# First loads and the slots of all operations rearranged, and the low halves of the FFN's relu outputs moved from VectorE to POOL, in a two-layer cross-attention kernel

## Chip, cores and metric

The kernel runs on one core of a Trainium2 chip. The metric is the device time of one execution in microseconds; the time of the kernel before is the median of 3 runs.

## What is computed

`x` (64 x 128 x 256, f32) goes through two layers, each a cross-attention and a feed-forward part, each on the layer-normed `x` and added to it:

```python
x = x + L0_xattn(_layernorm(x), ctx, ctx, mask, ...)
x = x + L0_ffn(_layernorm(x), W1, b1, W2, b2)
x = x + L1_xattn(_layernorm(x), ctx, ctx, _lenS2, ...)
x = x + L1_ffn(_layernorm(x), W_base, ..., Wa_up, ba_up)

def _quantize(W):                      # in L0_ffn, EPS = 1e-5
    gamma = jnp.mean(jnp.abs(W))
    return jnp.clip(jnp.round(W / (gamma + EPS)), -1.0, 1.0)
h = jax.nn.relu(jnp.einsum('bsd,fd->bsf', x, Wq1) + b1)
out = jnp.einsum('bsf,df->bsd', h, Wq2) + b2
```

Attention has 16 heads of 16 over 128 keys; layer 0 masks scores by an integer mask, layer 1 by a length for each sequence. The second feed-forward part has 8 experts: for each it reconstructs the input, takes the expert of the smallest loss for each sequence, and adds that expert's adapter to a dense base.

## The kernel before

The 64 sequences are worked in 32 pairs (256 rows of `x` each), and everything of a pair has one place in a fixed timetable. Each engine runs the same loop `for t in range(FIRST, END)`, with FIRST = -14 and END = 16 * 31 + 79, and in it lines `for p in at(t, o)`: operation `o` of pair `p` is issued in slot t = 16 p + o. So 16 slots are one pair's period, and up to six pairs are in work at once. Slots are an order and no clock: each engine runs its list in order, waits by semaphores (`Signal.done`), and a late operation holds all that stand behind it. The timetable is written out by hand for TensorE (PE), VectorE (DVE), ScalarE (ACT), GpSimd (POOL) and SyncE (SP, which issues all DMAs).

The stages of pair p and their slots on TensorE: keys and `count` -11, `turn(0)` (transpose of the normed x) -7, `queries(0)` -6, then by DMA through a scratch in DRAM (`spill`, `stack`) into `qs` and `ks`; `scores(0, j)` 0 to 7, `scores_t(0, j)` 6 to 13, `mix(0, u)` 9 to 15, `output(0)` 17, `turn(1)` 20, `ffn_up` 22 to 24, `ffn_down` 28 and 29, then the same attention for layer 1 from 33 to 58, experts from 61 on, `up` 75.

- Scores are made twice. `scores` goes to VectorE for the row maxima (`maximum`, L818; in layer 0 four custom instructions with the mask's bias, L831, in layer 1 one reduction, L823). `split_max` (L836) writes them as f16 pairs, `maxima` (L354) on SyncE puts these as two more rows into `qs` by four small DMAs, and `scores_t` (L1147), with the maxima in the product, goes to ACT for the exponential (`exps`, L593). In layer 0 POOL multiplies the result by the mask (`apply_mask`, L502) before `mix` (L1159).
- The first FFN wants its f32 activations as two f16 parts. `relus` (L616) on ACT writes `work` (two buffers), `h_highs` (L630) the f16 value, and `h_lows` (L882) on VectorE the rest, `work - high`. The relu of the third and fourth piece waits until both have read the buffer. Keys and queries are split in the same way (`high` on ACT, `low` on VectorE, L794).
- POOL also makes rstd and the normalised x of four stages (`rstd_of` L462, `normalise` L484), the mask's parts and bias, and adds the biases of two projections (`add_bias`).
- PSUM has one bank for scores, one for transposed scores, one for `mix`, and five for all else (`BANKS`, L54): each name there, as T0 (`turn(0)`), F1_0 to F1_3 (`ffn_up`), O0 (`output(0)`), lives in one bank, and TensorE may start a name only when the reader of the bank's last name is done.

Head: SyncE loads pair 0 and the EARLY weights, the lengths, the two FFN weights (1 MB each) and the fifteen LATE weights, then constant rows of `qs` and `ks` (nine DMAs from a DRAM row, L392 and L395), and only then enters the loop. VectorE sums |W| of the FFN weights at t = 0 (L1062), POOL reduces the sums over partitions (L556), and VectorE quantises in ten steps at t = 2 to 11 (`quantise`, L744).

Of the kernel before, what the change touches and what calls it, by code (L numbers as in the profile page):

```python
# [86 lines left out]
def build(nc, x, lens, mask, mask_t, wq0, bq0, wk0, bk0, wv0, bv0, wo0, bo0, w1t, b1, w2t, b2,  # L87
          wq1, wk1, wv1, wo1, w_base, wd1, bd1, wd2, bd2, adapters, ctx_in, out):
    with ExitStack() as ctx:
# [109 lines left out]
        const_dram = dram("const_dram", [3, T], F16)  # L199
# [79 lines left out]
        rows_loaded = sem("rows_loaded")  # L279
# [30 lines left out]
        def _(sp):  # L310
            def load(p, ahead=False):
                if p == 0 and not ahead:
                    return
# [19 lines left out]
            def stack(l, j, p):  # L333
# [7 lines left out]
                sp.wait_ge(scr_written[l][j], 16 * (p + 1))  # L341
                for n in range(4):
# [1100 lines left out]
```

## Time and profile before

| | us |
|---|---|
| median of 3 runs | 1799.05 |
| lowest, highest | 1795.69, 1802.66 |
| profiled execution | 1797.68 |
| its span | 1795.7 |
| TensorE busy | 1595.8 |
| VectorE busy | 1491.1 |
| ACT busy | 903.7 |
| POOL busy | 977.2 |

The profile is one execution. The span runs from its first to its last instruction, and the execution's own time is 2.0 us longer. Busy times are of instructions in work; an engine's sequencer and issued DMAs do not count. A view of waits says before which instruction an engine stood idle and what released it; where several semaphores are waited for, it names the one that came last by the profile, which can be the wrong one. `L` numbers are lines of the kernel before.

### The profile page before, as it was taken

The numbers are of one execution on the slowest core, as the hardware profiler recorded it, in microseconds if no ns is written. First come the engines' busy times: TensorE is split into PE (matmuls) and PEld (weight loads), VectorE is DVE, ScalarE is ACT, GpSimd is POOL, SyncE is SP. The second block draws the span as 40 slices with busy tenths as digits, with TensorE's granted clock in tenths as the row PEclk, the third lists the DMA queues.
The fourth block names the chain that finished last, engine by engine and source line by source line (L and its number), as shares of the span: only waits on it lengthen the run. The fifth ranks groups of instructions, "written<-read, shape, count | busy, mean of one in ns | idle before, by whom it ended". The sixth has DMA issues, their size and how long they took to land.

```text
span 1795.7 us, 44012 instructions
## 1 busy us (share of the span) xinstructions
PE 1595.8 (89%) x15136; PEld 1290.6 (72%) x15136; DVE 1491.1 (83%) x5215; ACT 903.7 (50%) x2465; POOL 977.2 (54%) x1069
## 2 busy tenths in 40 slices
PE   2467999999999999999999999999999999999875
PEld 1355777787777777877777778777777787777654
DVE  2667798988889998888899998888899989888652
ACT  0123455555555555555555655555556555555542
POOL 2456655655565656555666565556665655564200
PEclk9879999999999999999999999999999999999987
DMA  6345456554554564555545655555546555542311
GB/s 172 57 65 91 87 85 105 93 90 93 96 84 85 92 105 93 90 93 95 88 79 94 105 98 85 93 99 90 77 89 105 97 90 89 99 83 50 57 35 30
DMA packets 286501, 157.32 MB, mean 88 GB/s; under 512 B 38964, under 2 KB 281928, under 8 KB 286280
## 3 DMA queue, kind: packets, MB, share of 16 engines
q1 hardware_dynamic: 286280, 154.51, 49.1%
q8 instruction: 121, 1.98, 0.6%
q14 instruction: 100, 0.82, 0.2%
HBM read 111.44 MB, written 41.96 MB: 85 GB/s over the span
## 4 chain that ended last, share of the span: by engine, by line
PE 52%; DVE 26%; issue 10%; DMA 5%; SPq 4%; POOL 2%; ACT 2%; POOLq 0%; DVEq 0%; ACTq 0%
PE psD L1182 7%; DVE dump L831 6%; PE psD L1214 5%; PE psD L1203 5%; PE psV L1170 4%; PE psD L1224 4%; PE psD L1118 4%; PE psD L1129 4%; PE psS L1143 4%; PE psX L1155 4%; DVE dif L902 3%; PE psD L1248 3%; DMA qs<-scr 2%; PE psD L1089 2%; DVE hhl L884 2%
## 5 line engine op out<-in xcount | busy, mean ns | idle before, releaser
L603 ACT ACTIVATE pT<-psX 128x512 f32<-128x512 f32 x512 | 305.4, 596 | 406.1 <-PE psX L1155 404.6
L506 POOL TENSOR_TENSOR pT<-pT,keep 128x512 f32<-128x512 f32 x256 | 334.5, 1312 | 94.3 <-ACT pT L603 86.9
L465 POOL TENSOR_SCALAR veps<-mv 128x2 f32<-128x2 f32 x128 | 28.9, 226 | 589.7 <-DVE mv L776 589.7
L491 POOL TENSOR_SCALAR xn<-xr,mv,rstd 128x256 f32<-128x256 f32 x256 | 312.1, 1226 | 7.3 <-POOL rstd L475 0.2
L831 DVE CUSTOM_DVE_ANT_0 dump<-psS,bias 128x128 bf16<-128x128 f32 x1024 | 234.3, 284 | 40.3 <-PE psS L1143 39.1
L823 DVE TENSOR_REDUCE mx<-psS 128x4 f32<-128x512 f32 x256 | 173.2, 677 | 102.5 <-PE psS L1143 100.7
L1143 PE MATMUL psS<-ks,qs 65*128 65x128 f16 x2048 | 204.4, 223 | 56.5 <-DMA qs<-scr 38.0
L647 ACT ACTIVATE dif<-dif 128x256 f32<-128x256 f32 x512 | 206.5, 408 | 75.6 <-DVE dif L902 75.4
L902 DVE SCALAR_TENSOR_TENSOR dif<-psD,bd2s,xT 128x256 f32<-128x256 f32 x512 | 213.1, 470 | 14.3 <-PE psD L1224 13.6
L1155 PE MATMUL psX<-qs,ks 67*128 67x128 f16 x2048 | 201.9, 221 | 20.0 <-ACT pT L603 15.5
L1143 PEld LDWEIGHTS psS<-ks,qs 65*128 65x128 f16 x2048 | 146.1, 99 | 99.1 <-issue 29.4
L1155 PEld LDWEIGHTS psX<-qs,ks 67*128 67x128 f16 x2048 | 142.3, 98 | 70.8 <-ACT pT L603 27.8
L1170 PE MATMUL psV<-pT,v 128*32 128x128 f32 x4096 | 171.7, 287 | 14.0 <-POOL pT L506 10.7
L1224 PE MATMUL psD<-hd,wd2s 64*128 64x256 f32 x1024 | 144.9, 401 | 13.9 <-DVE xr L875 12.4
L1182 PE MATMUL psD<-wo,attT 128*128 128x256 f32 x512 | 138.5, 418 | 13.1 <-DVE attT L866 13.0
L1170 PEld LDWEIGHTS psV<-pT,v 128*32 128x32 f32 x4096 | 99.6, 112 | 60.8 <-issue 36.5
L627 ACT ACTIVATE work<-psD,b1s 128x256 f32<-128x256 f32 x256 | 104.4, 488 | 72.4 <-PE psD L1195 57.2
L1106 PE MATMUL psD<-ctxT,wk 128*128 128x256 f32 x512 | 125.1, 388 | 12.2 <-DVE bqr L938 12.2
L1195 PE MATMUL psD<-xs,w1q 128*128 128x256 f16 x1024 | 133.8, 274 | 0.1
L1118 PE MATMUL psD<-xT,wq 128*128 128x256 f32 x512 | 132.1, 395 | 0.7 <-ACT xT L576 0.7
L1129 PE MATMUL psD<-wv,ctxT 128*128 128x256 f32 x512 | 131.5, 401 | 0.0
L1089 PE MATMUL psD<-ident,xn 128*128 128x128 f32 x512 | 83.2, 286 | 54.0 <-ACT work L627 46.6
(101 smaller groups left out, 3177.1 us busy)
## 6 DMA issues: line engine op xcount, KB each, us to landing
scr<-packed SPq DMA_DIRECT2D x128, 256.0 KB, 2.8
ks<-scr SPq DMA_DIRECT2D x256, 128.0 KB, 4.5
qs<-scr SPq DMA_DIRECT2D x256, 128.0 KB, 4.6
adapter<-in_adapters SPq DMA_DIRECT2D x64, 192.5 KB, 2.7
xr<-in_x SPq DMA_DIRECT2D x32, 256.0 KB, 2.8
ctxT<-in_ctx SPq DMA_DIRECT2D x32, 256.0 KB, 3.1
qs<-mrows SPq DMA_DIRECT2D x512, 2.0 KB
out_y<-xr SPq DMA_DIRECT2D x32, 256.0 KB, 5.0
```

The lines of the kernel that those rows point to most:

```text
L491: nc.gpsimd.tensor_scalar(xn[:, XN[s], b], xr[:, p % NX, b], mv[:, s, b, 0:1], rstd[:, s, b:b + 1], ALU.subtract, ALU.mult).then_inc(norme ...
L506: nc.gpsimd.tensor_tensor(blk, blk, keep[:, p % 2, j // 4].unsqueeze(1).to_broadcast([P, 4, P]), ALU.mult).then_inc(masked.sem, 1)
L603: nc.scalar.activation(pT[:, j % 4], X[:], ACT.Exp, scale=SCALE).then_inc(exp_done[l].sem, 1)
L647: nc.scalar.activation(blk, blk, ACT.Square, accum_out=acc[:, e, b:b + 1]).then_inc(squared.sem, 1)
L831: ins = nc.vector.tensor_tensor_reduce(out=dump[:, a], in0=S[:, a * P:a * P + P], in1=bias0[:, p % 2, b], scale=1.0, scalar=-3e38, op0=ALU ...
L902: nc.vector.scalar_tensor_tensor(out=dif[:, e % 4, k], in0=bank[f"rec{e}"][:, k * T:k * T + T], scalar=bd2s[:, e, k:k + 1], in1=xT3[:, p % ...
L1118: ins = nc.tensor.matmul(dst[:, m * T:m * T + T], wq[l][:, k, m * P:m * P + P], src[:, k], start=(k == 0), stop=(l == 1 and k == KD - 1))
L1143: ins = nc.tensor.matmul(S[:, a * P:a * P + P], qs[0:MASK_ROW + 1, r, h, t0:t0 + P], ks[0:MASK_ROW + 1, r, h, t0:t0 + P], start=True, stop ...
L1155: ins = nc.tensor.matmul(X[:, a * P:a * P + P], ks[0:ROWS, r, h, t0:t0 + P], qs[0:ROWS, r, h, t0:t0 + P], start=True, stop=True)
L1170: ins = nc.tensor.matmul(V[32 * a:32 * a + 32, (2 * half + s) * P:(2 * half + s) * P + P], v2[l][:, b, half * UH + 2 * a + s], pT[:, (2 * ...
L1182: ins = nc.tensor.matmul(dst[:, b * D:b * D + D], attT[:, l, b, k], wo[l][:, k], start=(k == 0), stop=(k == KD - 1))
L1224: ins = nc.tensor.matmul(dst[s][:, k * T:k * T + T], wd2s[half, m, k * P:k * P + P], hd[half, m], start=True, stop=True)
```

## The change

Four things change at once.

1. *Head.* Pair 1 is loaded ahead (`load(1, True)`); the rows of constants in `qs` and `ks` are written by one memset on POOL and one on VectorE, each 3 partitions x 6144 words, in place of the nine DMAs; the LATE loads are issued inside the loop, one a slot from t = -4 on; the |W| sums, the length steps and the POOL reduction move from t = 0 to t = -6, the ten quantising steps from t = 2 to 11 together to t = -2.
2. *Slots.* Nearly every operation on all five engines has another slot or another place within it; END is 16 * 31 + 77.
3. *Banks.* The five shared PSUM banks hold other groups of names.
4. *Low halves.* `h_lows` is an instruction of POOL.

```diff
-END = BODY * (NP - 1) + 79
+END = BODY * (NP - 1) + 77
 BANKS = (
-    ("rec2", "cnt", "rec0", "rec7", "down", "up"),
-    ("rec4", "v0", "F1_1", "T2", "O1"),
-    ("O0", "k1", "T1", "rec5", "F2", "rec1", "loss"),
-    ("F1_3", "hd1", "rec3", "k0", "q1", "T3"),
-    ("q0", "v1", "T0", "rec6", "F1_0", "F1_2", "hd0"),
+    ("cnt", "rec5", "v1", "hd0", "q0"),
+    ("v0", "q1", "T2", "F1_1", "T0", "hd1", "T3"),
+    ("O0", "F1_2", "rec1", "loss", "rec7", "up"),
+    ("O1", "k0", "rec6", "rec3", "F2", "down", "rec0"),
+    ("rec2", "F1_0", "T1", "k1", "F1_3", "rec4"),
 )
...
-                for dst, src in LATE:
-                    sp.dma_start(dst, src).then_inc(w_late, 16)
-                sp.wait_ge(len_steps, 4)
-                sp.dma_start(len_dram, len_rows[:]).then_inc(len_stored, 16)
-                sp.wait_ge(len_stored, 32)
-                for n in range(NR):
-                    sp.dma_start(qs[MASK_ROW:MASK_ROW + 1, n], const_dram[1:2].unsqueeze(1).to_broadcast([1, H, T]))\
-                        .then_inc(rows_loaded, 16)
-                    for k in range(2):
-                        sp.dma_start(ks[MASK_ROW + 1 + k:MASK_ROW + 2 + k, n],
-                                     const_dram[2:3].unsqueeze(1).to_broadcast([1, H, T])).then_inc(rows_loaded, 16)
+            load(1, True)
...
+                if LATE_SLOT <= t < LATE_SLOT + len(LATE):
+                    dst, src = LATE[t - LATE_SLOT]
...
+                        sp.dma_start(dst, src).then_inc(w_late, 16)
...
+            nc.gpsimd.memset(qs[MASK_ROW:MASK_ROW + 3].rearrange("p r h t -> p (r h t)").bitcast(F32), pair16(BIG16))\
+                .then_inc(q_rows_set, 1)
...
+            def h_lows(p, j):
+                h_high.done(pool, p, j)
+                nc.gpsimd.tensor_tensor(hhl[:, 1, 2 * j:2 * j + 2], work[:, j % 2], hhl[:, 0, 2 * j:2 * j + 2],
+                                        ALU.subtract).then_inc(h_low.sem, 1)
...
-            def h_lows(p, j):
-                h_high.done(dve, p, j)
-                nc.vector.tensor_tensor(hhl[:, 1, 2 * j:2 * j + 2], work[:, j % 2], hhl[:, 0, 2 * j:2 * j + 2],
-                                        ALU.subtract).then_inc(h_low.sem, 1)
...
+            nc.vector.memset(ks[MASK_ROW:MASK_ROW + 3].rearrange("p r h t -> p (r h t)").bitcast(F32), pair16(M_UP))\
+                .then_inc(rows_set, 1)
...
-                for p in at(t, 23):
-                    h_lows(p, 0)
```

In the rows below every line is one instruction, or several alike, in the order in which the engine issues them, with the semaphores it waits for in brackets.

TensorE, from the last pieces of `ffn_up` (L1195) to `turn(0)` (L1089) and `mix` (L1170), before:

```order
L1195 MATMUL psD<-xs,w1q 128x256 [waits h_relu]
L1195 MATMUL psD<-xs,w1q 128x256 x7
L1143 MATMUL psS<-ks,qs 128x128 [waits stacked10,max_done0]
L1143 MATMUL psS<-ks,qs 128x128 x3
L1195 MATMUL psD<-xs,w1q 128x256 [waits k_low0]
L1195 MATMUL psD<-xs,w1q 128x256 x7
L1089 MATMUL psD<-ident,xn 128x128 [waits normed0,h_relu]
L1089 MATMUL psD<-ident,xn 128x128 x3
L1170 MATMUL psV<-pT,v_0 32x128 [waits masked,turned1]
L1170 MATMUL psV<-pT,v_0 32x128 x7
```

and now (L1130 keys, L1180 `scores_t`, L1168 `scores`, L1220 `ffn_up`, L1195 `mix`, L1113 `turn(0)`):

```order
L1130 MATMUL psD<-ctxT,wk 128x256 [waits ctx_loaded1,h_relu]
L1130 MATMUL psD<-ctxT,wk 128x256 x3
L1180 MATMUL psX<-qs,ks 128x128 [waits exp_done0]
L1180 MATMUL psX<-qs,ks 128x128 x3
L1168 MATMUL psS<-ks,qs 128x128 [waits stacked10,max_done0]
L1168 MATMUL psS<-ks,qs 128x128 x3
L1220 MATMUL psD<-xs,w1q 128x256 [waits loss_out]
L1220 MATMUL psD<-xs,w1q 128x256 x7
L1195 MATMUL psV<-pT,v_0 32x128 [waits masked,turned1]
L1195 MATMUL psV<-pT,v_0 32x128 x7
L1113 MATMUL psD<-ident,xn 128x128 [waits normed0,h_relu]
L1113 MATMUL psD<-ident,xn 128x128 x3
```

`mix` now stands ahead of `turn(0)`, and the fourth piece of `ffn_up` has moved behind it. The `h_relu` for which `turn(0)` waits was that of F1_2, the third piece; now it is that of F1_1.

POOL, from the first mask of layer 0 (L506, `apply_mask`) to the fourth or fifth, before:

```order
L506 TENSOR_TENSOR pT<-pT,keep 128x512 [waits exp_done0]
L459 TENSOR_SCALAR bias<-mqf,allc 128x128 [waits max_done0,mask_q]
L459 TENSOR_SCALAR bias<-mqf,allc 128x128
L506 TENSOR_TENSOR pT<-pT,keep 128x512 [waits exp_done0] x2
L498 TENSOR_TENSOR xr<-xr,bob 128x512 [waits normed0]
L498 TENSOR_TENSOR xr<-xr,b2b 128x512 [waits normed1]
L506 TENSOR_TENSOR pT<-pT,keep 128x512 [waits exp_done0]
```

and now (L523 `apply_mask`, L528 `h_lows`, L476 bias, L515 `add_bias`):

```order
L523 TENSOR_TENSOR pT<-pT,keep 128x512 [waits exp_done0] x2
L528 TENSOR_TENSOR hhl<-work,hhl 128x512 [waits h_high]
L476 TENSOR_SCALAR bias<-mqf,allc 128x128 [waits max_done0,mask_q]
L476 TENSOR_SCALAR bias<-mqf,allc 128x128
L523 TENSOR_TENSOR pT<-pT,keep 128x512 [waits exp_done0]
L528 TENSOR_TENSOR hhl<-work,hhl 128x512 [waits h_high]
L523 TENSOR_TENSOR pT<-pT,keep 128x512 [waits exp_done0]
L515 TENSOR_TENSOR xr<-xr,b2b 128x512 [waits normed1]
L515 TENSOR_TENSOR xr<-xr,bob 128x512 [waits normed0]
L528 TENSOR_TENSOR hhl<-work,hhl 128x512 [waits h_high] x2
L523 TENSOR_TENSOR pT<-pT,keep 128x512 [waits exp_done0]
```

Four low halves of the pair before stand between the first mask and the fifth, two of them back to back.

SyncE in the head, from the last row copies (L392, L395) to the first pair's stacks (L344), before:

```order
L392 DMA qs<-const_dram 1x16x256
L395 DMA ks<-const_dram 1x16x256 x2
L330 DMA scr<-packed 128x4x256 [waits k_low0,k_high0]
L344 DMA ks<-scr 16x16x256 [waits scr_written01]
L344 DMA ks<-scr 16x16x256 x3
L351 DMA ks<-const_dram 1x16x256
L330 DMA scr<-packed 128x4x256 [waits q_low0,q_high0]
L344 DMA qs<-scr 16x16x256 [waits scr_written00]
```

and now, from the early load of pair 1 (L327 to L334) on (L341 `spill`, L361 and L368 `stack`):

```order
L327 DMA xr<-in_x 128x2x256
L330 DMA ctxT<-in_ctx 128x512
L333 DMA mq_ld<-in_mask 128x2x128 [waits mask_k,mask_q]
L334 DMA mt_ld<-in_mask_t 128x2x128
L341 DMA scr<-packed 128x4x256 [waits k_low0,k_high0]
L361 DMA ks<-scr 16x16x256 [waits rows_set,len_stored,scr_written01]
L361 DMA ks<-scr 16x16x256 x3
L368 DMA ks<-const_dram 1x16x256
L341 DMA scr<-packed 128x4x256 [waits q_low0,q_high0]
L361 DMA qs<-scr 16x16x256 [waits scr_written00]
L361 DMA qs<-scr 16x16x256 x3
```

The spills of pair 0 now follow the loads of pair 1 directly; the LATE loads and the lengths' row come behind the second stack.

In the steady loop SyncE still issues `spill(0, 1, p + 1)` ahead of `maxima(0, p, 1)` (slots 9 and 10, before both 8), while on VectorE `low(0, 1, p + 1)` moves from before the eighth maximum, `maximum(0, p, 7)`, to behind the `split_max(0, p, 1)` that follows it.

## Rows read from the trace of the kernel before

**Rows 1.** The page, part 1: busy us (share) xinstructions
```profile
PE 1595.8 (89%) x15136; PEld 1290.6 (72%) x15136; DVE 1491.1 (83%) x5215; ACT 903.7 (50%) x2465; POOL 977.2 (54%) x1069
```

**Rows 2.** Windows: busy us of each engine, PEclk, DMA share, GB/s
```profile
913.27:937.15 23.88, 21.75 (x218) 18.11 (x216) 22.45 (x59) 12.56 (x28) 16.78 (x15) 1.00 0.47 67
800.00:1000.00 200.00, 189.65 (x1858) 154.86 (x1856) 179.69 (x625) 110.79 (x302) 121.26 (x132) 0.99 0.54 91
```

**Rows 3.** Timeline of TensorE: `count` of pairs 7 and 32
```profile
297.03 0.27 PE L1096 MATMUL psD<-mtb,onesb 128*128 128x256 bf16 x1
...
1577.86 0.27 PE L1096 MATMUL psD<-mtb,onesb 128*128 128x256 bf16 x1
```

**Rows 4.** The view of the waits from 500 to 1500 us: total, times, longest
```profile
POOL veps L465 <- DVE mv L776: 310.4, 58, 10.1
...
PE psD L1089 <- ACT work L627: 33.6, 20, 1.8
...
PE psD L1224 <- DVE xr L875: 7.9, 19, 0.4
```

**Rows 5.** Timelines of TensorE, ACT and VectorE, one steady pair
```profile
918.68 0.38 PE L1143 MATMUL psS<-ks,qs 65*128 65x128 f16 x4
...
921.56 0.65 PE L1089 MATMUL psD<-ident,xn 128*128 128x128 f32 x4 [1.62 <-ACT work L627]
...
925.58 0.39 PE L1155 MATMUL psX<-qs,ks 67*128 67x128 f16 x4
...
920.67 0.84 ACT L627 ACTIVATE work<-psD,b1s 128x256 f32<-128x256 f32 x2 [1.98 <-PE psD L1195]
...
915.96 0.82 DVE L800 SCALAR_TENSOR_TENSOR packed<-psD,bks,packed 128x256 f16<-128x256 f32 x2
...
917.66 0.98 DVE L838 TENSOR_SCALAR m<-mx 128x16 f16<-128x16 f32 x1
...
919.02 1.57 DVE L884 TENSOR_TENSOR hhl<-work,hhl 128x512 f16<-128x512 f32 x1
```

**Rows 6.** Timelines of SyncE's queue and of VectorE, head: first pair's spills
```profile
37.01 0.51 SPq L330 DMA_DIRECT2D scr<-packed  x1
...
41.90 0.53 SPq L330 DMA_DIRECT2D scr<-packed  x1
...
26.87 0.69 DVE L805 TENSOR_TENSOR packed<-psD,packed 128x512 f16<-128x512 f32 x1 [7.10 <-ACT packed L590]
```

**Rows 7.** Timelines of TensorE, VectorE and POOL, head: around the first scores
```profile
52.93 0.61 PE L1143 MATMUL psS<-ks,qs 65*128 65x128 f16 x4 [26.73 <-DMA qs<-scr]
...
54.43 2.28 DVE L1062 TENSOR_REDUCE gam<-dif 128x1 f32<-128x2048 f32 x1
56.62 2.28 DVE L1062 TENSOR_REDUCE gam<-hhl 128x1 f32<-128x2048 f32 x1
...
63.59 0.30 DVE L776 BATCH_NORM_AGGREGATE mv<-stats 128x2 f32<-128x6 f32 x2
...
66.38 0.89 POOL L449 TENSOR_SCALAR mqf<-mq_ld 128x256 f32<-128x256 int32 x1 [6.99 <-issue]
```

**Rows 8.** Timeline of VectorE, head: a memset
```profile
1.83 0.91 DVE L931 MEMSET v<- 128x1024 f32 x1 [0.16 <-issue]
```

**Rows 9.** Lines with shapes apart, 400 to 1600 us: busy, mean ns
```profile
L506 POOL TENSOR_TENSOR pT<-pT,keep 128x512 f32<-128x512 f32 x190 | 244.9, 1294 | 69.3 <-ACT pT L603 63.7
...
L884 DVE TENSOR_TENSOR hhl<-work,hhl 128x512 f16<-128x512 f32 x96 | 84.0, 896 | 0.0
...
L498 POOL TENSOR_TENSOR xr<-xr,bob 128x512 f32<-128x512 f32 x24 | 41.0, 1710 | 0.0
```

**Rows 10.** SyncE queue in a steady pair; chain of waits at 152 us
```profile
917.88 0.39 SPq L330 DMA_DIRECT2D scr<-packed  x1
919.12 2.69 SPq L358 DMA_DIRECT2D qs<-mrows  x4
...
152.50 1.70 DMA qs<-mrows
```

More of the change, by code:

```diff
@@ L311, in load @@
             def load(p, ahead=False):
-                if p == 0 and not ahead:
+                if p < 2 and not ahead:
                     return
@@ L693, in _ @@
                     exps(0, p, 0)
-                for p in at(t, -10):
+                for p in at(t, 22):
+                    relus(p, 0)
+                for p in at(t, -9):
                     high(0, 1, p)
@@ L1006, in _ @@
                     turn_out(1, p, 1)
-                for p in at(t, -9):
-                    low(0, 1, p)
                 for p in at(t, 7):
@@ L1039, in _ @@
                     split_max(1, p, 0)
+                for p in at(t, -4):
+                    low(0, 0, p)
+                for p in at(t, 12):
+                    turn_out(0, p, 0)
                 for p in at(t, 44):
@@ L1267, in _ @@
                     mix(1, p, 0)
-                for p in at(t, 33):
-                    turn(2, p)
+                for p in at(t, 49):
+                    scores_t(1, p, 3)
                 for p in at(t, 1):
@@ L1273, in _ @@
                     output(0, p)
-                for p in at(t, 49):
-                    scores_t(1, p, 3)
+                for p in at(t, 33):
+                    turn(2, p)
                 for p in at(t, 2):
                     scores(0, p, 2)
-                for p in at(t, 66):
-                    reconstruct(p, 2)
                 for p in at(t, 50):
@@ L1282, in _ @@
                     mix(1, p, 1)
+                for p in at(t, 66):
+                    reconstruct(p, 2)
                 for p in at(t, 3):
@@ L1288, in _ @@
                     queries(1, p)
+                for p in at(t, 68):
+                    reconstruct(p, 3)
+                for p in at(t, 52):
+                    mix(1, p, 2)
                 for p in at(t, 4):
                     scores(0, p, 4)
+                for p in at(t, 20):
+                    turn(1, p)
                 for p in at(t, 52):
                     scores_t(1, p, 6)
-                    mix(1, p, 2)
-                for p in at(t, 68):
-                    reconstruct(p, 3)
-                for p in at(t, 4):
+                for p in at(t, 5):
                     values(0, p)
-                for p in at(t, 20):
-                    turn(1, p)
+                for p in at(t, 53):
+                    scores_t(1, p, 7)
+                for p in at(t, -11):
+                    count(p)
                 for p in at(t, 5):
@@ L1303, in _ @@
                     keys(0, p)
-                for p in at(t, 53):
-                    scores_t(1, p, 7)
-                for p in at(t, -11):
-                    count(p)
-                for p in at(t, 6):
-                    scores(0, p, 6)
                 for p in at(t, 22):
@@ L1374, in _ @@
                     scores(1, p, 6)
-                    scores_t(1, p, 0)
                 for p in at(t, 62):
                     hidden(p, 0)
+                for p in at(t, 46):
+                    scores_t(1, p, 0)
+                for p in at(t, 47):
+                    scores(1, p, 7)
                 for p in at(t, 63):
```

267 lines of the change are left out of this document (143 added, 124 removed).

## The prediction

> **What bounds the kernel now.** I read the page first: TensorE is busy 89% of the span, VectorE 83% [rows 1]. Shares of a span hide its stages, so the windows come next. In the middle TensorE works 189.65 of 200 us at a granted clock of 0.99, its level of 2.4 GHz, while POOL works 121 [rows 2]. The `count` matmul is issued once a pair and gives the period: from the seventh pair's to the last one's are 25 periods in 1280.8 us, **51.23 us a pair** [rows 3]. At 189.65/200 TensorE's own work is 48.6 us of it, so at most 2.65 us a pair can be won in the steady part. Then the waits, over 1000 us or 19.5 pairs: TensorE stands 33.6 us for ACT's relu (1.72 us a pair) and 7.9 us for VectorE (0.4); POOL stands 310 us, 15.9 a pair, for moments [rows 4]. Last the timelines. The longest TensorE wait is that of the `turn(0)` transpose, 1.62 us [rows 5]. Its bank holds the relu's input, and the relu starts at 920.67, right behind the end of VectorE's low half (919.02 + 1.57). The view of the waits names TensorE as what released the relu, but the time fits the low half, which frees `work`. So a full VectorE queue, through ACT, stops TensorE once a pair.
>
> The head has its own limit. SyncE issues all fifteen LATE loads and the row copies ahead of the first spill, which goes only at 37.01, the second at 41.90, though VectorE had finished the second's data at 27.56 (26.87 + 0.69) [rows 6]. The first scores start at 52.93 after 26.73 us of idle. Then VectorE does two reductions (2.28 us each) between the maxima, and POOL, behind its all-reduce, stands 6.99 us for nothing that the profile shows before it prepares the second pair at 66.38; the second pair's moments had been ready at 63.9 [rows 7].
>
> **The change part by part.** The sum is made against the profiled execution, 1797.68 us (span 1795.7 and 2.0 around it); the median of the runs is 1.4 higher.
>
> *First scores.* LATE loads and row copies leave the way of the spills; rows of constants are set by memsets. The second spill can go at about 27.6 instead of 41.90, that is 14.3 us. VectorE's memset of 6144 words would take 6 x 0.91 = 5.5 us [rows 8], in a gap where it waits for the bias of the queries anyway. POOL's memset of the same size at the same price ends near 8 us, before the moments; at twice the price it would push the chain by 1 to 2 us, inside the lower end. The statistics no longer stand behind the length steps, which starts the query chain some 3 us earlier, but `any_of` and the gamma reductions (4.6 us) now stand before the low half of the queries on VectorE and hold most of that back. I take 1.2 us more: **15.5 us**. From spill to first scores stay 11.0 us (41.90 to 52.93). Ends: 9.3 us if the second MB-sized weight load and the early second pair slow the spills by 5 us; 17.3 if all 3 us come through. Quantising moves ahead of the first maxima, into that 11 us of DMA: its ten steps are cheap beside this, and its cover is just long enough.
>
> *Second pair.* The reductions (4.56 us) leave the maxima, and the 6.99 us stand falls into the time before the first scores. POOL will then start the second pair's rstd when its moments are ready rather than 4.3 us later (66.38 and two mask instructions, 1.8, against 63.9, [rows 7]). 4.56 + 4.3 = **8.9 us**; ends 4.6 and 11.5 (both stalls whole). LATE loads now come between later slots; their first user is the output projection of slot 17, so I cost them at nothing, covered by some 50 us. If that cover failed, the first FFN would wait.
>
> *Low halves to POOL.* VectorE loses 4 instructions of 0.896 us a pair, POOL gains 4. A POOL instruction with two SBUF inputs of this size takes 1.294 us [rows 9]: +5.2 us a pair on an engine with 15.9 idle. No trace row has it with an f16 input; ends 0.9 (VectorE's own time) and 2.6 us (twice the row), taken 1.3 since shape and form are the row's. The relus of slot 9 now wait for POOL's `h_lows`, which follows the mask of slot 7 directly, and the transpose's bank is held by F1_1, whose relu has no such wait; before the transpose TensorE has keys, scores, a further `ffn_up` and `mix`, over 3 us. So the 1.72 us wait goes: **-1.7 us a pair**. VectorE's 3.6 us by themselves are worth nothing more, since TensorE hardly waits for it otherwise.
>
> *What is late next.* SyncE's `maxima(0, p, 1)` stands behind the next pair's `spill(0, 1, p + 1)`, as before, but that waits for `low(0, 1, p + 1)`, which VectorE now does after `split_max(0, p, 1)` instead of before the last maximum. From the end of the eighth maximum (where the split starts, 917.66) to the landed rows: split 1.4 (to 919.02; 0.6 without the 0.8 of hold in it), low 0.8, spill 0.39, four issues 2.69, landing 1.70, together 7.0 us or 6.2 [rows 5, 10]. TensorE wants the rows for `scores_t(0, p, 4)`: before, 925.58 - 918.68 = 6.90 us behind `scores(1, p, 0)`, without its idle of 1.62 and some 0.4 it is 4.9; and `scores(1, p, 0)` came 1.0 us behind that maximum, and could come 0.2 behind it. So it will wait 6.2 - 1.0 - 4.9 = 0.3 at least and 7.0 - 0.2 - 4.9 = 1.9 at most; I take **+0.9 us a pair**. SyncE also gains: the store comes earlier and no longer stands just before the load that waits for it; nobody waited, so nothing.
>
> *Drain.* The count shrinks by two slots of 79. The last pair needs 1795.7 - 1577.9 = 218 us from its `count`, 2.5 us a slot; ends 0 and -5, taken 0, since the last chain is set by waits.
>
> **Sum**: 1797.7 - 15.5 - 8.9 - 27 x 0.8 = 1797.7 - 46.0 = **1752 us**, with 27 steady periods of 51.2 - 0.8 = 50.4. Its own range: the ends of the wait for the rows make the steady gain -0.2 to +1.4 a pair, so 1736 to 1779; the head's ends (13.9 and 28.8 us) move each by 4 to 10 us more.
>
> **Rivals.**
> *TensorE alone bounds.* The new slots leave no wait but 0.4 us: 49.0 a pair, 27 x 2.2 = 59.4; 1797.7 - 24.4 - 59.4 = 1714. For it: the largest wait goes. Against: the maxima above.
> *VectorE gives nothing back.* It stays full from slot 0 to 8, and POOL is busier while it works. The split at 917.66 took 0.98 us for 16 columns, the low half 1.57 against a mean of 0.90: VectorE's small instructions are held while POOL runs [rows 5, 9]. With POOL busy in all of slots 6 to 13 the split takes its worst 1.4 each time, and scale-outs likewise; one more 0.8 us on the way to the second scores and the gain is gone: 1797.7 - 24.4 = 1773. The Trainium skill (SBUF — State Buffer, Who interferes with whom) says that a VectorE instruction with two SBUF inputs contends with a GpSimd one that reads SBUF, and one of them blocks fully. By that rule each added POOL instruction holds what is left of such work on VectorE; the trace agrees so far as the 0.98 and 1.57 us go.
> *POOL becomes the bound; slower.* From `scores_t(0, p, 0)` at 913.27 to the fourth transpose at 937.15 TensorE is busy 21.75 us and POOL 16.78 [rows 2]. In the new order two masks fall behind the fourth stage's normalisation and four low halves come before it: 16.78 - 2 x 1.29 + 4 x 1.3 = 19.4 us, behind some 1.1 us of scores and exp, against TensorE's 21.5 without one `scores_t`. That leaves 1.0 us. From 1.55 us on, a low half costs TensorE 4 us for each us more. The kernel becomes slower where that outweighs 0.8 a pair and the head's 24.4 / 27 = 0.9, and 9 us more (0.3): 2.0 + 1.0 = 3.0 over four, so from 2.05 us on. At 2.6 us it is 5.2 - 1.0 - 0.8 = 3.4 a pair, 27 x 3.4 = 92, 1797.7 - 24.4 + 92 = 1865. For it: the tight place, and POOL's addition of the same size at 1.71 us in one slot [rows 9]; against: at 1.71 it would be +0.6 - 0.8 a pair, 1768, no loss. The Trainium skill (GPSIMD Engine Reference, Engine selection) speaks against the move: two-input elementwise work is about twice as slow there as on VectorE. By that figure and VectorE's 0.896 the low half would be 1.8 us and the time, with 2.0 - 1.0 - 0.8 a pair, 1779; the mask row's 1.294 is for the same shape and decides.
>
> **How the numbers follow.** Forecast 0.55, TensorE alone 0.15, VectorE gives nothing 0.20, POOL 0.10. The range 1716 to 1789 leaves out the deepest part of the second case and nearly all of the last. A measurement can tell 0.5%, 9 us. Faster (under 1790): 0.55 + 0.15 + 0.15 + 0.01 = 0.86. Same: the poor end of the third case 0.05 and 0.02 of the last, 0.07. Slower: the rest of the last, 0.07.
>
> **What would show it.** First scores near 37 to 38 us, the second pair some 24 us earlier; periods of `count` near 50.4; no wait of `turn(0)` for `work`; a wait of `scores_t` for `qs<-mrows` or a longer VectorE wait of about 0.9 us a pair; low halves on POOL of 1.3 us with POOL at about 36 of 50 us. Wrong: low halves of 1.9 us, the fourth transpose or `mix` waiting for POOL, or first scores after 44 us.

## The result and the profile after

| | before | after |
|---|---|---|
| median, us | 1797.37 (4 runs) | **1727.98** (4 runs) |
| lowest, highest | 1795.59, 1802.66 | 1724.99, 1730.12 |
| profiled execution, its span | 1797.68, 1795.7 | 1727.22, 1725.2 |

The ratio is 0.960, with a 95% interval of 0.957 to 0.963. The forecast of 1752 was 24 us too high; the range held the time.

Where did the 70.5 us of span go? The `count` matmul is issued once a pair and cuts the program into three. The timeline of TensorE after:

```profile
36.63 0.61 PE L1168 MATMUL psS<-ks,qs 65*128 65x128 f16 x4 [10.87 <-DMA qs<-scr]
...
47.02 0.27 PE L1120 MATMUL psD<-mtb,onesb 128*128 128x256 bf16 x1
...
274.54 0.27 PE L1120 MATMUL psD<-mtb,onesb 128*128 128x256 bf16 x1
...
1498.20 0.27 PE L1120 MATMUL psD<-mtb,onesb 128*128 128x256 bf16 x1
```

The three `count` lines are those of the second, seventh and 32nd pair. The last two answer to [rows 3], the scores to [rows 7].

| stretch | before | after | gain |
|---|---|---|---|
| to the seventh `count` | 297.03 | 274.54 | 22.5 |
| 25 periods | 1280.8 (51.23 each) | 1223.7 (**48.95** each) | 57.2 |
| last `count` to the end | 217.8 | 227.0 | **-9.2** |

So the head did what was expected, the steady part gave nearly three times as much (2.28 us a pair, not 0.8), and the drain took 9 us back.

The head after, timelines of SyncE's queue, of VectorE and of POOL:

```profile
20.92 0.37 SPq L341 DMA_DIRECT2D scr<-packed  x1
...
27.27 0.38 SPq L341 DMA_DIRECT2D scr<-packed  x1
...
4.88 5.18 DVE L959 MEMSET ks<- 3x6144 f32 x1 [1.23 <-issue]
...
2.25 5.21 POOL L458 MEMSET qs<- 3x6144 f32 x1
...
27.45 0.78 POOL L586 PARTITION_ALL_REDUCE gam<-gam  x2 [5.59 <-issue]
35.27 1.77 POOL L466 TENSOR_SCALAR mqf<-mq_ld 128x256 f32<-128x256 int32 x1 [7.05 <-issue]
```

The second spill goes at 27.27 instead of 41.90 [rows 6] and the scores start at 36.63 instead of 52.93. POOL's stand of 7 us is still there (7.05, before 6.99 [rows 7]), but now it ends before the first scores.

The steady part. First the page's busy times, then the window that answers to [rows 2] with its columns, then all waits of TensorE from 500 to 1500 us, which answer to [rows 4]:

```profile
PE 1584.5 (92%) x15136; PEld 1279.1 (74%) x15136; DVE 1316.8 (76%) x5086; ACT 891.8 (52%) x2465; POOL 1104.2 (64%) x1198
...
800.00:1000.00 200.00, 195.86 (x1941) 159.98 (x1938) 165.35 (x654) 113.77 (x318) 136.94 (x148) 1.00 0.54 99
...
PE psD L1207 <- DVE attT L898: 10.2, 20, 0.5
PE psS L1168 <- DVE mx L863: 8.2, 20, 0.5
```

TensorE works 195.9 of 200 us where it worked 189.65. The wait of `turn(0)` for the relu (33.6 us) is gone, and no wait for the maxima rows (`qs<-mrows`) stands in this stretch. What is left are two waits of VectorE's making: 0.5 us a pair of `output` (L1207) for the transposed attention output, 0.4 of `scores` (L1168) for a maximum.

The waits are not the whole gain. By the windows of the 25 periods, the same 11829 instructions of TensorE keep it busy for 1215.5 us before and 1197.8 us after, so of the 2.3 us a pair 0.7 is less busy time for the same work and 1.6 is less idling. The granted clock, 0.99 and 1.00, does not explain it: with the new banks alone (`e7_before_new_banks`, below) the clock was 1.00 and the busy time 1216.5 us. With the new slots and the old banks (`e12_old_banks_low_on_dve`) it was 1199.8 us. So most of this came with the slots; how is not shown. VectorE has 174 us less to do than in [rows 1], POOL 127 more.

The low halves on POOL, their neighbours and VectorE's small instructions, 400 to 1600 us, shapes apart; they answer to [rows 9]:

```profile
L523 POOL TENSOR_TENSOR pT<-pT,keep 128x512 f32<-128x512 f32 x193 | 243.4, 1267 | 77.0 <-ACT pT L633 75.2
L528 POOL TENSOR_TENSOR hhl<-work,hhl 128x512 f16<-128x512 f32 x97 | 115.1, 1196 | 7.7 <-ACT hhl L663 7.7
L515 POOL TENSOR_TENSOR xr<-xr,bob 128x512 f32<-128x512 f32 x23 | 29.1, 1266 | 0.0
...
L872 DVE SCALAR_TENSOR_TENSOR m<-mx,m 128x16 f16<-128x16 f32 x97 | 35.3, 364 | 3.3
L894 DVE TENSOR_TENSOR atok<-otok,rden 128x256 f32<-128x256 f32 x99 | 50.8, 513 | 3.4
```

A low half takes 1.20 us on POOL. And here is one steady pair, where it meets VectorE, by the timelines of VectorE, POOL and TensorE:

```profile
918.22 0.26 DVE L870 TENSOR_SCALAR m<-mx 128x16 f16<-128x16 f32 x1
918.51 1.08 DVE L872 SCALAR_TENSOR_TENSOR m<-mx,m 128x16 f16<-128x16 f32 x1
...
921.99 0.82 DVE L894 TENSOR_TENSOR atok<-otok,rden 128x256 f32<-128x256 f32 x1
922.84 0.45 DVE L898 STREAM_TRANSPOSE attT<-atok 128x256 f32<-128x256 f32 x1
...
918.40 1.16 POOL L528 TENSOR_TENSOR hhl<-work,hhl 128x512 f16<-128x512 f32 x1
919.66 1.52 POOL L476 TENSOR_SCALAR bias<-mqf,allc 128x128 f32<-128x128 f32 x2
921.26 1.27 POOL L523 TENSOR_TENSOR pT<-pT,keep 128x512 f32<-128x512 f32 x1
...
923.43 1.97 PE L1207 MATMUL psD<-wo,attT 128*128 128x256 f32 x8 [0.54 <-DVE attT L898]
```

The second step of the split (L872) starts 0.11 us behind POOL's first low half and ends with it; `atok` (L894) runs beside POOL's third mask and takes 0.82 us. Behind both stands the transpose for which TensorE waits 0.54 us. That was the first suspect.

### The profile page after: what moved, and what is told of

The parts are those of the page before. It is cut to its first block, busy times and chain, and to the rows that moved or that the text cites. A ratio compares the mean times of both kernels' runs of the same rounds, so it can differ in the third digit from the quotient of the medians.

```text
span 1725.2 us, 44058 instructions
## 1 busy us (share of the span) xinstructions
PE 1584.5 (92%) x15136; PEld 1279.1 (74%) x15136; DVE 1316.8 (76%) x5086; ACT 891.8 (52%) x2465; POOL 1104.2 (64%) x1198
## 4 chain that ended last, share of the span: by engine, by line
PE 47%; DVE 38%; issue 7%; DMA 3%; POOL 2%; ACT 1%; SPq 1%; DVEq 0%; ACTq 0%; POOLq 0%
DVE dump L863 11%; PE psD L1239 7%; PE psD L1228 7%; DVE dif L929 6%; PE psD L1207 4%; PE psD L1153 4%; PE psD L1273 4%; PE psS L1168 3%; PE psD L1142 3%; PE psV L1195 3%; PE psX L1180 3%; DVE atok L894 3%; PE psD L1249 3%; DVE otok L886 2%; DVE m L872 2%
## 5 line engine op out<-in xcount | busy, mean ns | idle before, releaser
L523 POOL TENSOR_TENSOR pT<-pT,keep 128x512 f32<-128x512 f32 x256 | 323.1, 1268 | 108.2 <-ACT pT L633 105.6
L929 DVE SCALAR_TENSOR_TENSOR dif<-psD,bd2s,xT 128x256 f32<-128x256 f32 x512 | 216.8, 472 | 63.6 <-PE psD L1249 63.5
L1168 PE MATMUL psS<-ks,qs 65*128 65x128 f16 x2048 | 202.6, 221 | 49.2 <-DVE mx L863 22.6
L1180 PE MATMUL psX<-qs,ks 67*128 67x128 f16 x2048 | 200.4, 220 | 15.5 <-ACT pT L633 8.7
L1168 PEld LDWEIGHTS psS<-ks,qs 65*128 65x128 f16 x2048 | 141.6, 98 | 97.8 <-issue 34.0
L1180 PEld LDWEIGHTS psX<-qs,ks 67*128 67x128 f16 x2048 | 141.6, 98 | 55.6 <-issue 18.6
L1195 PE MATMUL psV<-pT,v 128*32 128x128 f32 x4096 | 165.9, 280 | 8.0 <-POOL pT L523 4.3
L528 POOL TENSOR_TENSOR hhl<-work,hhl 128x512 f16<-128x512 f32 x128 | 151.5, 1193 | 11.9 <-ACT hhl L663 11.9
L1207 PE MATMUL psD<-wo,attT 128*128 128x256 f32 x512 | 132.1, 403 | 19.3 <-DVE attT L898 19.2
L1249 PE MATMUL psD<-hd,wd2s 64*128 64x256 f32 x1024 | 146.3, 405 | 2.0 <-DVE dif L929 2.0
L1195 PEld LDWEIGHTS psV<-pT,v 128*32 128x32 f32 x4096 | 96.8, 109 | 61.4 <-issue 39.3
L1220 PE MATMUL psD<-xs,w1q 128*128 128x256 f16 x1024 | 134.0, 274 | 1.4 <-DVE xs L911 0.8
L606 ACT ACTIVATE xT<-psD 128x512 f32<-128x512 f32 x96 | 57.1, 595 | 137.4 <-PE psD L1113 137.4
L1239 PE MATMUL psD<-xT,wd1s 128*128 128x256 f32 x512 | 126.0, 390 | 0.7 <-ACT xT L606 0.7
```

The source lines that it names most:

```text
L523: nc.gpsimd.tensor_tensor(blk, blk, keep[:, p % 2, j // 4].unsqueeze(1).to_broadcast([P, 4, P]), ALU.mult).then_inc(masked.sem, 1)
L929: nc.vector.scalar_tensor_tensor(out=dif[:, e % 4, k], in0=bank[f"rec{e}"][:, k * T:k * T + T], scalar=bd2s[:, e, k:k + 1], in1=xT3[:, p % ...
L1168: ins = nc.tensor.matmul(S[:, a * P:a * P + P], qs[0:MASK_ROW + 1, r, h, t0:t0 + P], ks[0:MASK_ROW + 1, r, h, t0:t0 + P], start=True, stop ...
L1180: ins = nc.tensor.matmul(X[:, a * P:a * P + P], ks[0:ROWS, r, h, t0:t0 + P], qs[0:ROWS, r, h, t0:t0 + P], start=True, stop=True)
L1195: ins = nc.tensor.matmul(V[32 * a:32 * a + 32, (2 * half + s) * P:(2 * half + s) * P + P], v2[l][:, b, half * UH + 2 * a + s], pT[:, (2 * ...
L1207: ins = nc.tensor.matmul(dst[:, b * D:b * D + D], attT[:, l, b, k], wo[l][:, k], start=(k == 0), stop=(k == KD - 1))
```

## The experiments

All kernels run beside the kernel before on the same chip, whose median there was 1798.7 to 1800.5 us. "Pieces" are the four low halves of a pair, 0 to 3. Periods are taken like above, from the seventh to the 32nd `count`.

### Where is the move worth something: low halves back, alone, and twice

The theory was that slots and banks bring the steady gain and the relief of VectorE little; the rival, that the relief brings it.

`e1_low_on_dve`, the changed kernel with its low halves back on VectorE:

```diff
-                h_high.done(pool, p, j)
-                nc.gpsimd.tensor_tensor(hhl[:, 1, 2 * j:2 * j + 2], work[:, j % 2], hhl[:, 0, 2 * j:2 * j + 2],
+                h_high.done(dve, p, j)
+                nc.vector.tensor_tensor(hhl[:, 1, 2 * j:2 * j + 2], work[:, j % 2], hhl[:, 0, 2 * j:2 * j + 2],
```

(pieces 0 to 3 in VectorE's slots 23, 25, 26 and 27)

> The changed kernel with only the four low halves of the FFN given back to VectorE, each at about the place that it had before (slots 23, 25, 26, 27). Theory A (the steady gain comes from slots and banks: the transpose's bank no longer hangs on a relu that waits for a low half; VectorE's relief is worth little): 1735 to 1750 us. Theory B (the steady gain comes from the 3.6 us a pair that VectorE loses): the steady 57 us are gone, the head's 22 stay, about 1775 to 1785.

Measured: **1707.03 us** (1703.38 to 1713.23), ratio 0.949 (0.946 to 0.953). The period is 48.24. Not only is the relief of VectorE worth nothing in the new order, the move to POOL costs 0.7 us a pair there.

`e2_before_low_on_pool`, the kernel before with this move alone (POOL's slots 23, 25, 26, 26):

> The kernel before with only the four low halves moved to POOL, one behind the second mask, one behind the third, two behind the fourth. Theory A: the third relu waits for POOL's low half as it did for VectorE's, so 1790 to 1805 us, no change. Theory B: the steady gain of 57 us appears without the rest, about 1740.

Measured: 1771.74 us (1769.23 to 1776.7), ratio 0.985 (0.982 to 0.988), period 50.09. The same move wins 1.14 us a pair in the old order. The waits of TensorE there, 500 to 1500 us:

```profile
PE psD L1089 <- ACT work L639: 17.0, 20, 0.9
PE psD L1182 <- DVE attT L878: 10.3, 20, 0.5
```

`turn(0)` waits 0.85 us a pair for the relu, where it waited 1.72 [rows 4]: half of that wait was VectorE's queue ahead of the low half.

`e3_before_new_head`, the kernel before with the new head and nothing else:

```diff
-                for dst, src in LATE:
-                    sp.dma_start(dst, src).then_inc(w_late, 16)
+            load(1, True)
...
-                if t == 0:
+                if t == GAMMA_SLOT:
...
-                if 2 <= t < 12:
-                    quantise(t - 2)
+                if t == QUANT_SLOT:
+                    for n in range(10):
+                        quantise(n)
```

> The kernel before with only the new head (early load of pair 1, memset rows, LATE loads in the loop, gamma sums at slot -6, quantising at -2); slots, banks and low halves as before. If the head's gain is its own and lasts to the end: 22 to 25 us, about 1773 to 1776. Rival: the new slots are needed for it (POOL and VectorE of the second pair): 1785 to 1790.

Measured: 1777.94 us (1776.57 to 1779.75), ratio 0.988 (0.986 to 0.990), period 51.20. The head is worth 22.6 us by itself, by the medians, and leaves the period alone; in its profile the second `count` comes 20.8 us earlier than before (48.85 for 69.63).

`e5_low_twice`, the changed kernel with each low half computed twice on POOL:

```diff
                 nc.gpsimd.tensor_tensor(hhl[:, 1, 2 * j:2 * j + 2], work[:, j % 2], hhl[:, 0, 2 * j:2 * j + 2],
+                                        ALU.subtract).then_inc(h_twice.sem, 1)
+                h_twice.done(pool, p, j)
+                nc.gpsimd.tensor_tensor(hhl[:, 1, 2 * j:2 * j + 2], work[:, j % 2], hhl[:, 0, 2 * j:2 * j + 2],
                                         ALU.subtract).then_inc(h_low.sem, 1)
```

> The changed kernel with each low half computed twice on POOL: 4 x 1.2 = 4.8 us a pair more, all before the fourth stage's normalisation. If POOL has the slack of 1.0 us a pair that I predicted: (4.8 - 1.0) x 27 = 103 us more, about 1830. If the slack is all of POOL's idle time (some 10 us a pair): 1728 to 1735.

Measured: 1841.82 us (1839.58 to 1842.72), ratio 1.023 (1.021 to 1.025): slower than before. The waits of TensorE, 500 to 1500 us:

```profile
PE psD L1232 <- POOL hhl L532: 37.6, 19, 2.0
PE psD L1117 <- POOL xn L509: 9.4, 8, 1.2
```

`ffn_down` and the fourth transpose now wait for POOL. The period grows by 3.68 us to 52.63 for 4 x 1.2 = 4.8 us more work, so POOL had 1.1 us a pair to spare.

### Is there a wait for the maxima rows

`e4_low_before_max`, the changed kernel with VectorE's `low(0, 1, p)` at slot -9, ahead of the eighth maximum, so that the spill and the rows behind it can leave earlier:

```diff
+                for p in at(t, -9):
+                    low(0, 1, p)
                 for p in at(t, 7):
                     maximum(0, p, 7)
                     split_max(0, p, 1)
-                for p in at(t, -8):
-                    low(0, 1, p)
```

> The changed kernel with VectorE's low half of the first packed piece (low(0, 1, p)) one slot earlier, ahead of the eighth maximum, so that the spill and the maxima rows behind it can leave earlier. If the maxima rows are what my prediction took them for (0.9 us a pair), this gives most of it back over 27 pairs: 1700 to 1712. If no such wait exists (the view of the waits of the changed kernel shows none of TensorE for these rows), nothing is gained, and the eighth maximum comes some 0.8 us later, for which the second scores already wait 0.4: 1728 to 1740.

Measured: 1729.99 us (1725.45 to 1730.55), ratio 0.961 (0.957 to 0.965), period 48.97. No change against the changed kernel, whose waits of TensorE show none for these rows: there is no such wait in the steady part.

### Slots or banks

`e6_old_banks` is the changed kernel with the old table of PSUM banks, `e7_before_new_banks` the kernel before with the new one, `e12_old_banks_low_on_dve` the new slots with the old banks and the low halves on VectorE (`e1_low_on_dve` with the old table). The edit is the table alone:

```diff
-    ("cnt", "rec5", "v1", "hd0", "q0"),
-    ("v0", "q1", "T2", "F1_1", "T0", "hd1", "T3"),
...
+    ("rec2", "cnt", "rec0", "rec7", "down", "up"),
+    ("rec4", "v0", "F1_1", "T2", "O1"),
...
```

> The changed kernel with the PSUM banks as they were, slots and all else new: the turn(0) transpose shares its bank with the third ffn_up again, whose relu now waits for POOL's low half. If the change of banks took the relu's wait off TensorE, the wait is back with 1.5 us a pair or more: 1765 to 1790. If the slots alone took it away, the time stays within 0.5% of the changed kernel: 1720 to 1736.

Measured: 1767.91 us (1767.33 to 1769.29), ratio 0.982 (0.978 to 0.986), period 50.65. The table is worth 1.70 us a pair in the new slots. But the waits of TensorE, 500 to 1500 us, are not the one that I had named:

```profile
PE psD L1120 <- DVE dif L929: 18.7, 20, 1.0
...
PE psD L1207 <- DVE attT L898: 12.8, 19, 0.7
...
PE psD L1249 <- ACT xT L606: 12.0, 20, 0.6
...
PE psD L1113 <- ACT work L657: 6.7, 19, 0.4
```

`turn(0)` (L1113) waits 0.34 us a pair for the relu. `count` (L1120), which shares a bank with the reconstruction `rec7` in the old table, waits 0.95 us for VectorE's difference, and a reconstruction (L1249) 0.6 us for the copy of a transposed x.

> The kernel before with the new table of PSUM banks and nothing else. If the banks alone free turn(0) of the relu, up to 1.7 us a pair over 31 pairs goes: 1747 to 1775. If the old slots put other work into a shared bank instead, the wait only changes its name and the time stays at 1790 to 1805.

Measured: 1812.62 us (1811.23 to 1817.3), ratio 1.008 (1.006 to 1.010): the table alone makes the old order slower, period 51.51. Its waits of TensorE, 500 to 1500 us:

```profile
PE psD L1129 <- DVE packed L805: 18.2, 20, 1.1
PE psD L1195 <- DVE packed L805: 14.3, 20, 0.7
PE psD L1239 <- DVE xr L875: 11.1, 20, 0.6
PE psD L1106 <- ACT work L627: 9.0, 20, 0.4
```

The wait of `turn(0)` has left this view, and four others of 2.7 us a pair in all stand in its place. One of them, L1106 of `keys`, is for a relu again.

> The new slots with the old PSUM banks and all low halves on VectorE (the new head stays). It completes the square: with the old slots and banks the move to POOL won 1.1 us a pair, with the new slots and banks it lost 0.7. If the loss hangs on the slots alone (piece 0 beside the split of the maxima), it is there with the old banks too: period 49.9 to 50.1 instead of 50.65, time 1747 to 1755. If the win hangs on the banks (turn(0) behind the relu that waits for VectorE's low half), it comes back: period 51 or more, 1775 to 1795.

Measured: 1749.14 us (1745.83 to 1750.28), ratio 0.972 (0.968 to 0.975), period 49.97. So with the old banks, too, the low halves on POOL cost 0.68 us a pair in the new slots, and the wait that they add is the same:

```profile
PE psD L1121 <- DVE dif L922: 18.6, 20, 0.9
PE psD L1250 <- ACT xT L594: 12.0, 20, 0.6
PE psD L1114 <- ACT work L645: 7.1, 20, 0.4
```

These are the rows of `e6_old_banks` without the one for `attT`. The square of periods:

| slots | banks | low halves on VectorE | on POOL |
|---|---|---|---|
| old | old | 51.23 | 50.09 |
| old | new | 51.51 | not run |
| new | old | 49.97 | 50.65 |
| new | new | 48.24 | **48.95** (the change) |

Read along one path, the slots bring 1.26 us a pair, the banks 1.73, and the low halves on POOL take 0.71 back.

### Which low half costs, and how

`e8_two_on_pool`, `e9_first_on_dve` and `e10_second_on_dve` leave some pieces on POOL and give the others to VectorE (piece 0 in slot 23, piece 1 in 25), with a semaphore for each engine's share. `e9_first_on_dve` for instance:

```diff
-        h_low = signal("h_low", KF // 2)
+        h_low = signal("h_low", 3)
+        h_lowv = signal("h_lowv", 1)
...
-                for p in at(t, 23):
-                    h_lows(p, 0)
...
+            def h_lows(p, j):
+                h_high.done(dve, p, j)
+                nc.vector.tensor_tensor(hhl[:, 1, 2 * j:2 * j + 2], work[:, j % 2], hhl[:, 0, 2 * j:2 * j + 2],
+                                        ALU.subtract).then_inc(h_lowv.sem, 1)
...
+                for p in at(t, 23):
+                    h_lows(p, 0)
...
+                h_lowv.done(pe, p)
```

> The changed kernel with the low halves of pieces 0 and 1 back on VectorE (slots 23 and 25) and those of pieces 2 and 3 left on POOL. With all four on VectorE it took 1707, with all four on POOL 1728. If the loss comes from what POOL's pieces 0 and 1 hold on VectorE in the slots between the scores and the output matmul, this is near 1707 to 1711. If it comes from POOL's later pieces, right ahead of the third normalisation, it stays at 1724 to 1730. If it is POOL's total work that counts, halfway: 1714 to 1720.

Measured: **1702.16 us** (1701.62 to 1711.73; the profile is of the slowest of its five runs), ratio 0.945 (0.942 to 0.949), period 48.26. Pieces 2 and 3 on POOL cost nothing.

> The changed kernel with the low half of piece 0 alone on VectorE, pieces 1, 2 and 3 on POOL. In the trace of the changed kernel POOL's piece 0 runs beside VectorE's split of the maxima (0.9 us instead of 0.2) and pushes POOL's third mask onto VectorE's atok (0.8 instead of 0.4); both stand ahead of the transposed attention output that TensorE waits 0.5 us for. If piece 0 is the cause, the period falls from 48.95 to 48.2 to 48.4 and the time is 1702 to 1712. If it is the number of pieces on POOL, it stays halfway between 1728 and 1702: 1717 to 1722.

Measured: 1707.63 us (1703.4 to 1710.63), ratio 0.948 (0.945 to 0.951), period 48.29.

> The changed kernel with the low half of piece 1 alone on VectorE, pieces 0, 2 and 3 on POOL. Piece 0 still holds the split and pushes the third mask: if it is the cause, the period stays 48.8 to 49.0 and the time 1722 to 1732. If it is the number of pieces on POOL, it is near 1717 to 1722, and if piece 1 was the cause, 1702 to 1712.

Measured: 1726.7 us (1725.4 to 1729.15), ratio 0.960 (0.956 to 0.963), period 48.94. So it is piece 0 alone: whatever the others do, the period is 48.2 to 48.3 with piece 0 on VectorE and 48.9 with it in this place on POOL. The place in `e8_two_on_pool`, by the timelines of VectorE, POOL and TensorE (the pair of the rows above; here `count` lies 5.63 us earlier):

```profile
912.59 0.25 DVE L866 TENSOR_SCALAR m<-mx 128x16 f16<-128x16 f32 x1
912.88 0.17 DVE L868 SCALAR_TENSOR_TENSOR m<-mx,m 128x16 f16<-128x16 f32 x1
...
913.22 0.65 DVE L912 TENSOR_TENSOR hhl<-work,hhl 128x512 f16<-128x512 f32 x1
...
916.05 0.42 DVE L890 TENSOR_TENSOR atok<-otok,rden 128x256 f32<-128x256 f32 x1
916.51 0.45 DVE L894 STREAM_TRANSPOSE attT<-atok 128x256 f32<-128x256 f32 x1
...
912.91 1.54 POOL L476 TENSOR_SCALAR bias<-mqf,allc 128x128 f32<-128x128 f32 x2
914.58 1.28 POOL L523 TENSOR_TENSOR pT<-pT,keep 128x512 f32<-128x512 f32 x1
...
917.10 1.97 PE L1212 MATMUL psD<-wo,attT 128*128 128x256 f32 x8
```

The split's second step takes 0.17 us instead of 1.08. POOL's third mask ends at 915.86, before `atok`, which takes 0.42 instead of 0.82. VectorE reaches the end of the transpose 4.37 us after the start of the split, with a low half of 0.65 us done on the way; in the changed kernel it took 5.07 us without it. These 0.70 us are as much as the periods differ by (0.69). The Trainium skill (SBUF — State Buffer, Who interferes with whom) says that a VectorE instruction with two SBUF inputs contends with a GpSimd one that reads SBUF. The traces agree where POOL's instruction has two inputs as well: both held instructions are of that kind, beside a low half and a mask.

They do not where POOL's has one tensor input. In the lines above VectorE's low half (L912) runs wholly beside POOL's mask bias (912.91, 1.54 us for two) and takes 0.65 us, no longer than with POOL idle; so do all 27 that start beside a bias between 100 and 1650 us. In the changed kernel 57 `atok` that start beside POOL's normalisation (`xn`, one tensor input) take 0.42 to 0.48 us, and 28 that start beside a mask 0.64 to 1.54.

`e11_first_behind_mask` keeps all four on POOL, but puts piece 0 behind the third mask, beside piece 1:

```diff
-                for p in at(t, 23):
-                    h_lows(p, 0)
...
                 for p in at(t, 24):
+                    h_lows(p, 0)
                     h_lows(p, 1)
```

> The changed kernel with all four low halves on POOL, but that of piece 0 behind the third mask instead of ahead of it. By the cause named for piece 0 (it runs beside the split and pushes the mask), both holds go, unless piece 0 now runs beside atok: period 48.2 to 48.5 and 1702 to 1715. If atok is then held by piece 0 in place of the mask, half comes back: 1712 to 1722. If the third relu on ACT waits for the late piece 0 and TensorE with it, nothing is won: 1724 or more.

Measured: 1747.98 us (1747.46 to 1748.63), ratio 0.971 (0.968 to 0.974), period 49.64; worse than the changed kernel, as the third of the cases expected. Timelines of ACT, POOL and TensorE:

```profile
939.01 0.84 ACT L656 ACTIVATE work<-psD,b1s 128x256 f32<-128x256 f32 x2 [2.73 <-PE psD L1219]
...
937.60 1.34 POOL L528 TENSOR_TENSOR hhl<-work,hhl 128x512 f16<-128x512 f32 x1
...
941.92 0.40 PE L1179 MATMUL psX<-qs,ks 67*128 67x128 f16 x4 [0.99 <-ACT pT L632]
```

The wait for `attT` is gone from TensorE's list. But the third relu has to wait until POOL's low half has freed `work` at 938.94 (the view names TensorE, whose third piece was done at 936.48), it stands in ACT's queue ahead of an exponential, and `scores_t` waits 1.0 us for that. So on POOL piece 0 has no good place: early it holds the split, late it holds the relu.

### The drain

No kernel was made for the drain; its rows come from the profiles above. `e6_old_banks` has the slots and the low halves of the changed kernel, and a drain of 216.5 us against 227.0. The windows of the second halves, the changed kernel first, then `e6_old_banks`, then the kernel before:

```profile
1611.70:1725.20 113.50, 78.15 (x505) 57.33 (x503) 45.66 (x128) 39.27 (x139) 10.33 (x13) 0.75 0.16 32
...
1657.40:1765.70 108.30, 74.65 (x545) 56.09 (x543) 46.76 (x131) 39.13 (x139) 12.85 (x16) 0.82 0.18 36
...
1686.80:1795.70 108.90, 75.52 (x546) 57.52 (x544) 47.91 (x136) 39.12 (x139) 13.72 (x17) 0.83 0.17 36
```

Over the whole drain TensorE is busy 185.8 us for 1540 instructions in the changed kernel and 175.9 for 1537 in the other, 9.9 of the 10.5 us between them. The granted clock in the last half is 0.75 against 0.82, 0.83 in the kernel before, whose TensorE was busy 176.2 us in its drain. Single instructions show the two levels of 1.2 and 2.4 GHz: the eight matmuls of `output`, 1.97 us at 923.43, take 3.78 here (timeline of TensorE, changed kernel):

```profile
1680.60 3.78 PE L1207 MATMUL psD<-wo,attT 128*128 128x256 f32 x8 [2.82 <-DVE attT L898]
```

What differs before the drain is TensorE's busy share in the steady part, 0.98 against 0.95. That the one causes the other is not shown: `e1_low_on_dve`, with 0.99, had 0.81 and a drain of 220.5 us. A single profile does not give the drain to better than some 3 us either: `e4_low_before_max`, as fast as the changed kernel and different in one operation's place, had 0.78 and 223.7.

## Why the prediction was right or wrong

- **First scores, -15.5 us: right.** They came 16.3 us earlier (52.93 to 36.63). The spill was expected at 27.6 and went at 27.27; VectorE's memset took 5.18 us for 5.5, POOL's ended at 7.46 for "near 8".
- **Second pair, -8.9 more: a little high.** The sum of 24.4 us measured 22.6 at the second `count` (69.63 to 47.02) and 22.5 at the seventh; alone the head gave 22.6 by the medians (`e3_before_new_head`). That POOL's stand would fall into the time before the first scores was right.
- **Low half of 1.3 us on POOL: right**, 1.20. The addition's 1.71 us was no price of POOL: the same instruction takes 1.27 in its new slot. The Trainium skill (GPSIMD Engine Reference, Engine selection) has two-input elementwise work about twice as slow there. Against VectorE's unheld 0.65 us (L912 above) that is 1.8 times, which agrees; my 1.8 us from it failed because VectorE's 0.896 us was a held duration.
- **`turn(0)`'s wait goes, -1.7 us a pair: right in the trace, incomplete in the reason.** Bank and slots were said to do it. Each does: the new table in the old slots removes it, and the new slots with the old table leave 0.34 us. But the new table alone trades it for 2.7 us of others, so the wait that goes is not what is won. And in the old slots the move to POOL alone takes half of it, which the prediction did not price.
- **VectorE's relief is worth nothing by itself: right in the new order, and too kind.** The move costs 0.71 us a pair there, in all 21 us of time. In the old order it won 29 us (`e2_before_low_on_pool`), which I had not separated.
- **Wait for the maxima rows, +0.9 us a pair: wrong, and the step that failed most.** I had TensorE want the rows 4.9 us behind `scores(1, p, 0)`, a distance of the old order. In the new one TensorE has an `ffn_up` and a `scores` more there: from 919.07 to 925.46 are 6.39 us, 5.85 without the wait for `attT`. The rows are also there sooner than the 7.0 us that I gave them from the start of the split. It starts at 918.22 and their issue ends at 923.79. My 1.70 us for the landing, read at 152 us, is too much here: in `e1_low_on_dve` and `e8_two_on_pool` the issue ends at 916.27 and 917.87, and `scores_t(0, p, 4)` starts at 917.54 and 919.13 without a wait, so the landing takes at most 1.27 us there. With that it is 6.8 us at most, and TensorE asks 7.24 us behind the start of the split. `e4_low_before_max` shows that nothing is to be had.
- **TensorE's own work, kept at 48.6 us a pair: wrong.** It came out at 47.9, and these 0.7 us are a third of the steady gain. Idling fell by 1.6 us a pair, near the 1.7 of the term above. So the 0.8 of the forecast lacked the 0.9 that was taken off for the rows, and these 0.7. The table of banks, worth 1.7 us a pair in the new slots, had no term of its own.
- **Drain, 0: wrong by +9.2 us.** Two slots fewer were weighed, the clock was not. By luck it hid a quarter of the steady part's error, and the head's 1.9 us a little more; without them the time would have been about 1717, at the lower end of the range.
- **Rivals.** *TensorE alone bounds* forecast 49.0 a pair, and 48.95 came: it was nearest in mechanism too, as no long wait is left. That the number fits so well is luck: its 48.6 of work and 0.4 of wait were 47.9 and 1.0. Its 1714 lacks the drain's 9.2 us, 1.9 of the head and 2.2 in the steady part (27 periods at 2.2 for 25 at 2.3). *VectorE gives nothing back* named the right mechanism (the split held by POOL) with the wrong price: 0.7 us a pair, on the way to `output`. Of the two durations that it rests on, the 1.57 us is of an instruction with two SBUF inputs. The 0.98 us is of one with a single input (L838), so it does not bear out the rule quoted there; it was held all the same, and ended at 918.64, just behind POOL's mask (918.61 by POOL's timeline). *POOL becomes the bound* had the slack right, 1.0 for 1.1 us, and the way it fails, which `e5_low_twice` shows: at 2.4 us a piece the kernel is slower than before.

Summed: 25 periods gave 57.2 us where 27 had been put at 21.6, which takes 35.6 from the forecast's 1752, and the head and the drain give back 1.9 and 9.2: 1727.

## What to carry to other kernels

An order that puts POOL's two-input instructions beside VectorE's small two-input ones has a price, here 0.9 us for the split and 0.4 for `atok`; POOL's one-input instructions had next to none. Look which of the held ones lies on the way to TensorE, and give that piece back: with piece 0 alone on VectorE the kernel took 1708 us, with two pieces there 1702, with all four 1707, which the intervals don't part, and with none 1728. The worth of one move (+1.1 or -0.7 us a pair) and of one table of banks (-0.3 or +1.7) changed sign with the order around it, so price it in the new order. Distances between two operations on an engine have to be counted in the new order as well.

## What the runs showed of the hardware that was not expected

- The drain's granted clock differed between nearly equal programs, 0.75 in the last half of the changed kernel and 0.82 in `e6_old_banks`, and the drain was 10.5 us longer at the lower one. What set the clock is open.
- Beside POOL's two-input instructions VectorE's small instructions were held (the split's second step 1.08 us for 0.17, `atok` 0.82 for 0.42). Beside its one-input ones they were hardly held: between 100 and 1650 us of the changed kernel the same two took at most 0.33 and 0.48 us there.
- POOL stood 5.59 us ahead of its partition reductions at 27.45 and 7.05 us behind them, while they took 0.78 themselves. Of the first stand at most 1.8 us were until VectorE's first sum (23.70); the rest and all of the second answer to nothing that the profile shows. In the head before, where POOL had idled 33.74 us ahead of its first reduction, only the second is seen [rows 7].
- A memset of 3 partitions x 6144 words took 5.18 us on VectorE and 5.21 on POOL, about what [rows 8] give for as many words on each of 128 partitions (6 x 0.91): few partitions don't make it cheaper.
